# A fourth place for the projections' rows, and five quads' layer norm inside the attention, in a macaron transformer block

## What is computed

```python
x = x + 0.5 * ffn(layernorm(x), ...)
x = x + attention(layernorm(x), ...)
x = x + 0.5 * ffn(layernorm(x), ...)

def ffn(h, ...):
    scores = softmax(h @ gate_w.T).transpose(0, 2, 1)      # 16 experts
    topk_w, topk_idx = top_k(scores, 256)                  # each expert takes 256 tokens of a batch
    x_tok = take(h, topk_idx)
    eo = ((gelu(x_tok @ Wg.T) * (x_tok @ Wu.T)) @ Wd.T) * topk_w
    out = zeros.at[topk_idx].add(eo)                       # the scatter
    return out + (gelu(h @ Ws_g.T) * (h @ Ws_u.T)) @ Ws_d.T
```

## Time and profile before

| | us |
|---|---|
| device time, median of 3 runs (1650.1 to 1656.79) | 1650.28 |
| device time of the profiled execution | 1650.51 |
| its span, first to last instruction | 1648.7 |
| PE / ACT / DVE / POOL busy in the span | 1508.1 / 994.2 / 862.7 / 564.2 |
| first expert stage | 0 to about 495 |
| projections | about 495 to 615 |
| attention | 617.20 to 1155 |
| second expert stage | 1155.78 to 1648.7 |

### The profile page before, as it was taken

One profiled execution on the slowest core, in us unless ns is written; L12 is line 12 of the kernel. 1 busy time (PEld: TensorE's weight loads), 2 busy tenths in 40 slices (PEclk: granted clock), 3 DMA queues, 4 the chain that ended last, 5 costly groups with the idle time before them and its releaser, 6 DMA issues. The chain is left out here.

```text
span 1648.7 us, 26498 instructions
## 1 busy us (share of the span) xinstructions
PE 1508.1 (91%) x9943; PEld 1047.6 (64%) x9945; DVE 862.7 (52%) x1848; ACT 994.2 (60%) x1358; POOL 564.2 (34%) x497
## 2 busy tenths in 40 slices
PE   4999999999976858999999999998499999999997
PEld 3788888888865633333333333333378888888886
DVE  6887676676636740123022032122688767666663
ACT  7322254544516748999999999997732225454541
POOL 3000256656546862111111021110300025665654
PEclk9999999999998988999999999999799999999999
DMA  8221266667635797315136245000722126766653
GB/s 277 71 90 52 66 168 152 157 147 152 152 39 177 213 241 162 56 24 79 31 49 116 77 68 73 7 14 33 274 71 90 52 66 169 152 158 145 152 132 39
DMA packets 121744, 183.14 MB, mean 111 GB/s; under 512 B 19664, under 2 KB 83152, under 8 KB 118480
## 3 DMA queue, kind: packets, MB, share of 16 engines
q1 hardware_dynamic: 92432, 130.04, 31.1%
q0 software_dynamic: 29184, 51.40, 14.9%
HBM read 125.82 MB, written 55.57 MB: 110 GB/s over the span
## 5 line engine op out<-in xcount | busy, mean ns | idle before, releaser
L1764 ACT ACTIVATE 8052_pr<-8052_pS 128x1024 f32<-128x1024 f32 x448 | 421.2, 1073 | 17.2 <-PE 8052_pS L1685 15.9
L1715 PE MATMUL 8052_pO<-8052_pr,6208_vres 128*32 128x512 f32 x1792 | 240.3, 606 | 5.9 <-DVE 8052_tO L1789 3.7
L1685 PEld LDWEIGHTS 8052_pS<-sq_rows,sk_rows 50*128 50x128 f32 x896 | 74.5, 185 | 213.9 <-ACT 8052_pr L1764 153.8
L1685 PE MATMUL 8052_pS<-sq_rows,sk_rows 50*128 50x512 f32 x896 | 185.3, 466 | 24.1 <-DMA sq_rows<-shift 19.6
L1789 DVE STREAM_TRANSPOSE 8052_tO<-8052_pO 128x512 f32<-128x512 f32 (+1 forms) x33 | 23.0, 698 | 312.2 <-PE 8052_pO L1715 312.2
L171 PE MATMUL 111_pGU<-columns_XT,weights_wts 128*128 128x512 f32 x384 | 152.5, 397 | 1.6 <-DVE columns_XT L864 1.6
L171 PE MATMUL 14727_pGU<-columns_XT,weights_wts 128*128 128x512 f32 x384 | 152.5, 397 | 1.6 <-DVE columns_XT L864 1.6
L1778 POOL TENSOR_SCALAR_AFFINE_SELECT 8052_pr<-8052_pr 128x512 f32<-128x512 f32 x32 | 21.4, 668 | 380.2 <-ACT 8052_pr L1764 380.2
L172 PE MATMUL 14727_pGU<-columns_XT,weights_wts 128*128 128x512 f32 x384 | 149.8, 390 | 0.0
L172 PE MATMUL 111_pGU<-columns_XT,weights_wts 128*128 128x512 f32 x384 | 149.8, 390 | 0.0
L173 PE MATMUL 111_pGU<-columns_XT,weights_wts 128*128 128x512 f32 x384 | 149.8, 390 | 0.0
(11 more groups left out here) (348 smaller groups left out, 3332.9 us busy)
## 6 DMA issues: line engine op xcount, KB each, us to landing
token_table<-weights_xn POOLq DMA_DIRECT2D x16, 512.0 KB, 6.4
111_raw_g<-WgT SPq DMA_DIRECT2D x16, 512.0 KB, 4.0
111_raw_u<-WuT SPq DMA_DIRECT2D x16, 512.0 KB, 3.6
111_raw_d<-WdT SPq DMA_DIRECT2D x16, 512.0 KB, 4.0
q_rows<-rows_half SPq DMA_DIRECT2D x32, 256.0 KB, 3.5
k_rows<-rows_half SPq DMA_DIRECT2D x32, 256.0 KB, 3.4
sq_rows<-q_rows SPq DMA_DIRECT2D x32, 256.0 KB
sk_rows<-k_rows SPq DMA_DIRECT2D x32, 256.0 KB
```

The source lines that it names most:

```text
L1685: m = t_.matmul(to[:, e, :], key, query, start=True, stop=True)
L1715: m = t_.matmul(pO[e * 32:(e + 1) * 32, off:off + wd], vres[:, (g // GB) * TPB + kt, at:at + 32], from_(e), start=n == first[j], stop=n == ...
L1764: s_exp.done(a.activation(to, pS[:, u % RING, :, :], ACT.Exp, scale=HD ** -0.5))
```

## The change

1. The ring `half` gets four places (`ROWS_RING = 4`), and the third `turns` buffer an allocation of its own. The low parts of the last three units (13, 14, 15) are made by VectorE and no longer by POOL (`POOL_LOW`).
2. Group 0's heads are loaded after the stores of units 8, 9, 10 and 11 (before: after units 9, 11, 11 and 13), and its shift rows with them (before: first thing in the attention).
3. The attention makes the second expert stage's layer norm for quads 0 to 4 (`READY = 5`): when a quad's last piece has been added, SP stores it at once, VectorE makes statistics, an inverse square root by four Newton steps and the normalised rows, in place in `acc`, in slots that avoid block ends by a margin (`quiet`), and SP stores these to the token table. Quads 0 to 3 are loaded back from the table into `xn_ahead` when group 6 is done with its buffer.
4. SP's list in the attention is ordered by slots. It no longer waits at the end for the stores to land; these waits move into the second expert stage.
5. The second expert stage loads no x: quads 5 to 7 are normalised there from `acc`. It gets the shared weights' high parts from POOL (before: ScalarE), and its lists on ScalarE and VectorE have a new order.
6. The memory layout of the expert stage is rearranged so that these buffers outlive the block change.

The core of the diff, shortened:

```diff
@@ projections, SP @@
-        J, W, KS = NQ, 4 * P, 3
+        J, W, KS = NQ, 4 * P, ROWS_RING
+            POOL_LOW = 2 * J - 3
                 def store(n):
                     q, a_ = n // 2, n % 2
-                    sp.wait_ge(*s_lo.at(n + 1))
+                    if n < POOL_LOW:
+                        sp.wait_ge(*s_lo.at(n + 1))
+                    else:
+                        sp.wait_ge(*s_last.at(n - POOL_LOW + 1))
...
-                    store(2 * q)
-                    store(2 * q + 1)
-                    for hh in {4: (0,), 5: (1, 2), 6: (3,)}.get(q, ()):
-                        sp.wait_ge(*s_clear.at(3))
-                        self.load_head(sp, 0, hh)
-                sp.wait_ge(*s_zero.at(1))
+                    for half_ in range(2):
+                        store(2 * q + half_)
+                        if q in (4, 5):
+                            sp.wait_ge(*s_clear.at(3))
+                            sp.wait_ge(*s_zero.at(1))
+                            self.load_head(sp, 0, 2 * (q - 4) + half_)
+                            self.load_shift(sp, 0, 2 * (q - 4) + half_)
@@ projections, VectorE, ahead of the flag @@
+                for n in range(POOL_LOW, 2 * J):
+                    self.s_rows[n % KS].wait(v, n // KS)
+                    low(n)
                 largest(J - 1)
@@ projections, POOL @@
                 for n in range(2 * J):
                     turned(n)
-                    if n >= 1:
+                    if 1 <= n <= POOL_LOW:
                         low(n - 1)
-                low(2 * J - 1)
@@ attention, plan @@
+            heads_at = {over[g - 2] - RING: g for g in range(2, NG)}
+            for m in range(READY):
+                store_at[done_at[m] + 1] = m
+                stats_at[quiet(done_at[m] + 1, 3)] = m
+                root_at[quiet(max(stats_at) + 3, 5)] = m
+                norm_at[quiet(max(max(root_at) + 5, done_at[m] + 14), 3)] = m
+                table_at[max(norm_at) + 3] = m
+            ahead_at = over[NG - 2] - 1
@@ attention, SP @@
-                for hh in range(GH):
-                    self.load_shift(sp, 0, hh)
...
+                def normalized(m):
+                    sp.wait_ge(*self.s_norm.at(m + 1))
+                    self.s_table.done(sp.dma_start(table[m], mine_of(m)))
+                    if m < 4:
+                        sp.wait_ge(*self.s_table.at(m + 1))
+                        residual(4 + m)
+                for w in range(NW):
+                    if w in heads_at:
+                        heads(heads_at[w])
+                    if w in store_at:
+                        store(store_at[w])
+                    if w in table_at:
+                        normalized(table_at[w])
+                    if w == ahead_at:
+                        sp.wait_ge(*s_S.at(over[NG - 2] + 1))
+                        for q in range(AHEAD):
+                            self.s_ahead.done(sp.dma_start(self.xn_ahead[:, q, :, :], table[q]))
+                for m in range(READY, 8):
                     store(m)
-                for k in range(4):
-                    sp.wait_ge(*s_out[k].at(2))
@@ attention, VectorE @@
+                def inverse_root():
...
+                    for _ in range(4):
+                        link(v.tensor_tensor(square[:, :], root[:, :], root[:, :], ALU.mult))
+                        link(v.tensor_tensor(square[:, :], square[:, :], half_var[:, :], ALU.mult))
+                        link(v.scalar_tensor_tensor(root[:, :], square[:, :], 1.5, root[:, :], ALU.add, ALU.mult))
+                    link(v.scalar_tensor_tensor(shift[:, :], mv[:, :, 0], -1.0, root[:, :], ALU.mult, ALU.mult))
+                def normalize(m):
+                    s_out[m % 4].wait(v, m // 4 + 1)
+                    for j in range(4):
+                        i = v.tensor_scalar(mine_of(m)[:, j, :], mine_of(m)[:, j, :], root[:, j:j + 1], shift[:, j:j + 1], ALU.mult, ALU.add)
+                    self.s_norm.done(i)
                 for n in range(NW):
+                    if n in stats_at:
+                        statistics(stats_at[n])
+                    if n in root_at:
+                        inverse_root()
+                    if n in norm_at:
+                        normalize(norm_at[n])
@@ expert stage, ScalarE @@
+                    if ready:
+                        if q >= 1:
+                            columns(q - 1)
+                        if 1 <= q <= J - ready:
+                            normalize(ready + q - 1)
+                        if 1 <= q < J - ready:
+                            deviation(ready + q)
@@ expert stage, VectorE @@
+                if ready:
+                    statistics(ready)
+                    statistics(ready + 1)
+                    scale(ready)
+                    low_columns(0)
+                    statistics(ready + 2)
+                    scale(ready + 1)
+                    low_columns(1)
+                    low_columns(2)
+                    scale(ready + 2)
+                    for q in range(3, J):
+                        if q == J - 1:
+                            softmax_in(0)
+                        low_columns(q)
@@ expert stage, POOL @@
+                def split_shared(w):
+                    if ready:
+                        s_raw[w].wait(g, 1)
+                        s_wh.done(g.tensor_copy(weight(1, w, 0), raw[w][:, :, :]))
+                    s_wh.wait(g, w + 1)
+                    split_lo(g, 1, w, s_wls)
...
-        prog.ffn(prog.x2, out)
+        prog.ffn(prog.x2, out, ready=READY)
```

More of the change, by code:

```diff
@@ L506, in _ @@
                 for q in range(J):
-                    if q >= first:
+                    if q >= first and not ready:
                         load_x(q)
@@ L1027, in _ @@
                         for k in range(KN):
[L1028 removed]
+                            s_stored[k].wait(g, kept[k])
                         gather(J)
@@ L1482, in load_head @@
         if hh == 0:
-            for n in range(3):
-                units = 2 * NQ // B if g < 4 else 2 * NQ
-                self.s_rows[n].wait(sp, (units - n + 2) // 3)
+            for n in range(ROWS_RING):
+                self.s_rows[n].wait(sp, self.stored(2 * NQ // B if g < 4 else 2 * NQ, n))
         head, loaded = g * 4 + hh, self.s_ld[k][pair]
```

254 lines of the change are left out of this document (166 added, 88 removed).

## The result

| | before | after |
|---|---|---|
| device time, median of four runs, us | 1653.53 | 1636.22 |
| the four runs, us | 1650.1 to 1656.82 | 1632.61 to 1644.13 |
| ratio | | 0.9896, 95% interval 0.9873 to 0.9919 |
| profiled execution, us (its span) | 1650.51 (1648.7) | 1644.13 (1642.4) |

The change makes the kernel faster by about 1%, 17.2 us by the ratio; a second measurement, the first of the experiments, gives 14.6. The forecast was 21.4 us, 1629.1. The profiled execution of after is the longest of its four, so it shows 6.4 us and not 17; the table further down therefore sets several executions side by side.

A forecast was written before the change was run, and what follows sets the result against it. TensorE bounds the expert stages, ScalarE's exponentials the attention; the change targets two seams where TensorE nearly idles. 1650.51 − 10.9 (seam one) + 4.5 (attention) − 15.0 (seam two) = 1629.1 us, range 1621 to 1638.

The forecast's parts named there:

- Seam one, 10.9 us: Projections to attention: earlier low parts, stores and shift loads bring the first exponential to about 611.2, gaining 10.9 us.
- POOL's turning ends about 601.0: End of projections: unit 15's turning, no longer behind a low part, ends about 601.0 instead of 602.9.
- the rule: VectorE and POOL exclude each other on their shared port pair; unit 15's low part would end about 605.9, 1.1 us later.
- Unit 11's landing: End of projections: unit 15's high part waits for unit 11's store, estimated landed at 602.5, bounds 601 and 607.
- SP now issues at 2.5 us each: End of projections: stores 13, 14, 15 issued back to back from 599.7, the last ending at 607.3 instead of 614.94.
- Rival A: Seam between projections and attention: queue fills, head 3 or unit 11's store lands 5 us late; gain 6, 1634.0; chance 0.14.
- The attention, 4.5 us lost: Quad 1's store behind group 5's 20 loads delays VectorE's turn and TensorE 3.9 us, slot 269 0.6; bounds 1 and 8.
- Seam two, 15.0 us: Attention to second expert stage: first product at 1182.0 instead of 1197.08, gaining 15.0 us, bounds 9 and 18.
- The dropped wait: End of attention: SP no longer waits for the last store, so the expert stage starts at 1153.1, gaining 2.7 us.
- Rival B: Second expert stage: TensorE restarts at 1.2 GHz and transposes and logits don't raise the clock; 1637.4; chance 0.12.
- one of the prediction's signs of being wrong: Second expert stage: the prediction is wrong if the clock is still 1.2 GHz when the first products run.
- Rivals C and D: C: layer norm stalls attention every time, 1664.6, chance 0.02. D: expert start gains only 2.7, 1641.4, chance 0.06.

The follow-up runs named there:

- the first of the experiments: The changed kernel measured and profiled once more, with no edit; median 1645.04 us beside 1658.08 for before, ratio 0.9912.
- seam one only: The changed kernel without layer norm in the attention (`READY = 0`) and with SP's old list there; 1643.21 us, ratio 0.9936 to before.
- POOL later: The changed kernel with one wait added: POOL splits the shared weights only after VectorE has made quad 7's shift; ratio 0.9878 to before.

## Why the prediction was right and where it was wrong

The side, the range and the three places of gain and loss were right; the saving was put at 21.4 us and is 17.2 or 14.6 us by the two measurements of the changed kernel. In absolute time 3 of the 7 us between 1629.1 and 1636.22 are not the change: the kernel before itself took 1653.53 beside it, and not 1650.51. The rest lies in two terms of the sum, seam one and the attention.

**Seam one, 10.9 us.** The attention's start was put 11.3 us behind the last rotation and the first exponential 12.8; the shortest seen is 13.24. Gains against the 23.69 of before are 5.0 to 9.9 us in the seven kernels with this code up to the first exponential, 7.7 in the mean. Three steps of it:
- "POOL's turning ends about 601.0": it ended at 602.65, where it ended before. This step is wrong. The Trainium skill (SBUF — State Buffer, SBUF: two separate sides) says that the port pair of VectorE and GpSimd is locked for a whole instruction and not shared; the rows agree, since 1.28 us became 2.18 and 2.24, and VectorE's low part 2.29 instead of 1.21; with the low parts back on POOL the turning took 1.25 again. The prediction had put 1.1 us on the rule; about half of that was needed: where no landing holds it, the low part of unit 15 ends 6.87 us behind the rotation, where the prediction had 6.4 and the rule 7.5.
- Unit 11's landing, estimated at 602.5, which is 4.1 us behind the rotation, with bounds 601 and 607, was 605.9 in after. In the seven kernels with this code it came 4.0 to 7.6 us behind the rotation, and in five of them the high part of unit 15 waited for it last; in two (seam one only, POOL later) it held nothing. So the estimate lay at the good end of its bounds, and this is the larger part of what is missing in after: the low part of unit 15 ended at 608.31, 10.1 us behind the rotation instead of 6.4.
- "SP now issues at 2.5 us each": 4.80, 5.09 and 3.76 us. This step is mis-sized too, and it is the smaller part: the last issue ended at 613.10, 2.3 us later than a 2.5 us issue behind that low part would have, and 0.5 to 1.8 us later in the six others. What held SP back is not shown; the DMA share of 1.02 can't be the whole reason, since before the issues took 2.5 us beside it. Rival A, which named unit 11's landing, gave 6 us instead of 10.9 and was the better number for this execution. The Trainium skill (DMA: Bandwidth & Descriptors, Queues, rings and completion order) says that SP's and ScalarE's queues have their rings on the same sixteen DMA engines; that a second issuing engine left the time as it was agrees with it.

**The attention, 4.5 us lost.** The place, the cause and the single stall were right, and so was the landing: 17.1 us against 16.3. The scaling took 2.31 us instead of 1.3, beside POOL's masks. The missing term is TensorE's clock: it was 1.00 until the pause of 4.56 us and 0.50 behind it, until about 913, and ScalarE, without reserve, waited another 2.8 us (the four gaps at 908 to 915). In the six kernels with this order the stall cost 7.4 us in the mean, where 3.9 had been put, and the statistics at slot 269 cost 0.9, where 0.6 had been put. The whole attention took 525.6 to 535.3 us, 5.2 to 14.9 more than before, 10.2 in the mean; the rest of that is a clock that fell elsewhere too (last section), which is not the stall's doing.

**Seam two, 15.0 us.** From the last exponential on, the five kernels with this code gained 11.5 to 17.5 us against 506.2, 14.9 in the mean. The dropped wait gave 2.8 (predicted 2.7). The first product was put 28.9 us behind the stage's start and came after 30.8 in after, 26.8 to 29.0 in four others. My chain had the normalisation of quad 7 ahead of the columns of quad 3, rightly; it had neither the shift held by POOL nor the clock's later falls. POOL's weights were covered, as said: the last subtraction ended at 1176.4. Of the steps at half clock one was read short: the logits' 1.75 us comes from a stretch at 0.68, and at 0.50 throughout they take 2.05 (after, at 1177.85). Rival B was half right. TensorE did start the stage at 1.2 GHz, but what B feared, that the transposes would not bring the clock up, did not happen: in after it rose at 1161.7, when TensorE had run nothing but transposes since 1156.6, and 2.7 us ahead of the first logits (1164.44). It then fell again in the gap at 1172 to 1176 (0.50 in 1176 to 1182) and a third time at 1189.05, so the first products ran at 0.61 us. By the letter this is one of the prediction's signs of being wrong; its cause was pauses inside the stage and not the slow start. In three of the four other executions with this code the first product took 0.40 us.

**Rivals C and D** are out: the normalisation of four of the five quads stalled nothing, and seam two gave 11.5 to 17.5 us and not 2.7.

## What to carry to other kernels

Where a step waits in order on an engine that others need, look at what its data stand behind on their queue; moving one store ahead of twenty loads took the stall away. A pause of TensorE can cost more than its own length, when its clock falls behind it and the engine beside it has no reserve. Where a DMA share near 1 stands in a window, give every landing there a range: under one code seam one took 13.75 to 18.65 us. Two executions of one kernel can differ by more than the edit, so a second profile of the same kernel belongs to the first experiments.

## What the runs showed of the hardware

- A VectorE step on 128x4 elements with two inputs in SBUF, 0.16 us by itself, was shown as busy for 1.19 to 2.38 us where it met POOL's subtraction of 128x1024, and for 0.69 to 0.71 where it met POOL's copy of 128x1024; it ended with POOL's step within 0.03 us (1172.20 and 1172.18 in after). Low columns, which read one input from PSUM, took their 1.28 us beside the same subtraction (at 1165.51 in after).
- The same pause of TensorE inside the attention, 1.58 us at 957.8 in before and 1.57 us at 960.9 in after, left the clock at 1.00 in the one and was followed by 0.50 in the other; in the kernel with seam one only, which has no layer norm there, it fell as well. In after ScalarE's gaps behind it were 2.6 us longer than in before. All fourteen profiles of the table have this pause, near exponential 356, and one of 1.54 to 1.57 us near exponential 84; the clock went to 0.50 behind the one in five of them and behind the other in five, partly different ones. What decides it is open.
